# Half tiles of 128 rows and a lead of four groups in the routed stage of a graph and expert kernel

## The chip, the cores and the metric

The kernel runs on one core of one Trainium2 chip. The metric is the device time of one launch in microseconds, the median of a few runs; smaller is better. Beside the timed runs there is one profiled execution, with a trace of every instruction and transfer, from which all rows below come.

## The reference

```python
x = x + gnn(layernorm(x), edges, ...)      # two RGCN layers over 10000 nodes, 5000 edges, 512 wide
x = x + moe(layernorm(x), ...)             # on every one of the 10000 rows:
#   shared = gelu(t @ sw1.T + sb1) @ sw2 ...           2 shared experts, 64 wide each
#   top_v, top_i = top_k(softmax(t @ gate_w.T + gate_b), 2)       of 8 experts
#   routed = sum over the two picked experts of top_v * (gelu(t @ rw1[e].T + rb1[e]) @ rw2[e] + rb2[e])
```

The change lies wholly in the second line, the experts.

## The kernel before

The graph layers are not touched. Then comes the routed stage. The 10000 rows are handled twice: as 20 **groups** of 512 rows (128 partitions x QT = 4), in order of the nodes, and as **tiles** of 256 rows (FW), in order of the experts that they need.

A group q is loaded from x (`load_group`, SyncE's queue SP), z, the result of the graph layers, is added to it by an accumulating transfer (`add_z`, GpSimd), and it gets its statistics (`q_stats`, VectorE), its root (`group_rstd`, GpSimd), its normalisation (`q_norm`, ScalarE, L1336), its transposes (`q_transpose`, TensorE, L1593) and its router logits. VectorE finds the two experts of each row (`route_a`, `route_b`), which of six **kinds** (pairs of neighbouring experts, `KINDS`) the row belongs to (`sort_kinds`), and from counts made on TensorE its place (`positions`). Then `sort_rows` scatters the rows to `sorted_rows` in DRAM, one region a kind (L1119, four scatters a group).

A tile is 256 consecutive rows of one kind. `pick_tile(i)` (VectorE) chooses the kind of which most rows are ready and writes four integers to `pick_int`: the first row, the slot of the up weights in a chain of eight expert pairs (`CHAIN`), and two chunks of the down weights. There are always NF = 45 tiles, as many as the worst split over six kinds can need. `load_tile` reads them by a register (L846, L847). TensorE turns the tile (`turn_tile`, L1637, L1633), multiplies it by the picked up weights (`up_routed`), and by the shared ones (`up_shared`). ScalarE takes the gelu (L1372), VectorE multiplies it by the rows' shares (`weigh`, L2184), TensorE turns the result (`turn_hidden`, L1670), ScalarE and VectorE split it into a high and a low part (`routed_hi`; `routed_lo`, which writes grl, L2193), and TensorE multiplies it by the down weights (`down_first`, `down_routed`). `store_tile` scatters the rows to the output. All multiplications go through the helper at L1467, three for each product.

Slot i of the loop `for i in range(NF)` holds tile i and, on each engine in an order written out by hand, steps of a group some way ahead: even slots count, turn and normalise, odd ones route (`turned_in_slot`, `routed_in_slot`, `ranked_in_slot`). The first LEAD_GROUPS = 5 groups are done ahead of the loop. Four of them have the buffers stage0q to stage3q, the fifth has stage4q, which lies over the tile buffers xt2 and xt3; so `load_tile(2)` waits for the sort of group 4. Ahead of its first gelu ScalarE has `q_norm(5)`.

On TensorE the registers are loaded inside the slot, between the turn of the shares ("x") of the next tile and the last product of this one:

```python
                down_routed(i, 0, chunks)                 # waits for s_grl
                if exists(i + 1):
                    turn_tile(i + 1, "x")
                    chosen = picked(i + 1)                # three value_loads, L1737
                down_routed(i, 1, chunks)
```

The two calls are the two halves (128 rows each) of the tile; both use the same slot and chunks. `weigh` is called twice a slot, once for each chunk, on both halves at a time; VectorE loads its two chunks by registers too (L2258).

## Time and profile before

| | |
|---|---|
| runs, us | 1600.15, 1600.99, 1612.06; median 1600.99 |
| profiled execution, us | 1598.47, of which its span is 1596.7 |
| mean granted TensorE clock | 0.98 of full |
| busy, of the span | TensorE 93%, VectorE 58%, ScalarE 44%, GpSimd 41% |

The span runs from the first to the last instruction of the trace. "Idle before, releaser" in a row is the time for which an engine stood ahead of an instruction and what ended it; "issue" means that nothing the profile shows was waited for. PE is TensorE's matmuls, PEld its weight loads, PEldq and SPq the instructions in the queues of TensorE and SyncE. PEclk is the granted TensorE clock in tenths or shares of full speed, 2.4 GHz.

### The profile page before, as it was taken

The page shows a single profiled execution, that of the slowest core. Times are in us where ns is not written, and L with a number is a line of the kernel's source. Part 1 is how long each engine was busy: PE and PEld are TensorE (multiplying, and loading weights), DVE is VectorE, ACT ScalarE, POOL GpSimd, SP SyncE. Part 2 cuts the span into 40 slices and gives each one's busy share as a digit, 9 for nine tenths or more (in the row PEclk, how much of TensorE's full clock was granted, in tenths as well). Part 3 has the DMA queues.
Part 4 walks back from the last instruction along what each step waited for, and adds up shares of the span by engine and source line. Part 5 has one row for each costly group of instructions (what it writes and reads, how often), then busy time and mean ns, then how long its engine had stood idle before and what let it go on. Part 6 is the DMA issues. An engine that isn't in the chain of part 4 may idle for free. (4 is left out here: it accounts for less than half of the span.)

```text
span 1596.7 us, 27768 instructions
## 1 busy us (share of the span) xinstructions
PE 1491.6 (93%) x8680; PEld 1200.0 (75%) x8680; DVE 927.9 (58%) x2667; ACT 705.7 (44%) x1231; POOL 662.6 (41%) x989
## 2 busy tenths in 40 slices
PE   6999998989898999999999986599999999999997
PEld 4777666777786677777888864478888888888986
DVE  5555686867752333334766556566666767665453
ACT  3334334556652212122666535446565656453322
POOL 3762232457753000000467634546546464543222
PEclk9999999999999999999999998699999999999999
DMA  9999999597757999999667688879776776534220
GB/s 243 277 279 286 298 294 304 190 289 131 128 91 170 295 290 279 278 292 272 157 126 133 106 214 175 236 204 249 224 233 191 221 213 200 167 129 131 93 75 3
DMA packets 130212, 325.95 MB, mean 204 GB/s; under 512 B 17115, under 2 KB 17641, under 8 KB 129698
## 3 DMA queue, kind: packets, MB, share of 16 engines
q1 hardware_dynamic: 84626, 211.19, 44.8%
q0 software_dynamic: 45456, 113.12, 31.1%
q8 instruction: 70, 1.15, 0.3%
q14 instruction: 60, 0.49, 0.1%
HBM read 205.62 MB, written 121.74 MB: 205 GB/s over the span
## 5 line engine op out<-in xcount | busy, mean ns | idle before, releaser
L1207 ACT ACTIVATE th<-bank 128x512 fp32r<-128x512 f32 x158 | 94.2, 597 | 291.7 <-PE bank L1487 291.6
L1005 POOL DMA_INDIRECT gx<-y,dst_slot x42 | 46.2, 1101 | 266.1 <-ACT xn_e L1227 243.0
L1842 DVE SCALAR_TENSOR_TENSOR tl<-bank,th 128x512 fp32r<-128x512 f32 x79 | 54.4, 689 | 162.3 <-ACT th L1207 162.0
L1139 POOL DMA_INDIRECT out<-xt,out_row x90 | 93.2, 1035 | 128.4 <-DVE xt L2198 92.3
L1467 PE MATMUL bank<-root2h,th 128*128 128x512 f32 x316 | 133.1, 421 | 12.6 <-DVE tl L1842 7.8
L1467 PE MATMUL bank<-root1h,th 128*128 128x512 f32 x316 | 131.6, 416 | 7.9 <-DVE yout L1869 4.8
L1869 DVE TENSOR_TENSOR yout<-bank,bias_b 128x512 f32<-128x512 f32 x150 | 102.3, 682 | 45.4 <-DMA y<-yout 18.7
L1467 PE MATMUL bank<-root2l,th 128*128 128x512 f32 x316 | 126.0, 399 | 0.0
L1467 PE MATMUL bank<-root2h,tl 128*128 128x512 f32 x316 | 125.2, 396 | 0.0
L1467 PE MATMUL bank<-root1l,th 128*128 128x512 f32 x316 | 125.0, 396 | 0.0
L1467 PE MATMUL bank<-root1h,tl 128*128 128x512 f32 x316 | 124.1, 393 | 0.0
L1845 DVE TENSOR_TENSOR tl<-bank,th 128x512 fp32r<-128x512 f32 x79 | 54.3, 687 | 85.3 <-ACT th L1207 84.9
L1467 PE MATMUL bank<-w1qh,tth 128*128 x360 | 102.2, 284 | 1.6 <-issue 1.6
L1467 PE MATMUL bank<-w1ql,tth 128*128 x360 | 102.4, 284 | 0.0
L1467 PE MATMUL bank<-w1qh,ttl 128*128 x360 | 102.1, 284 | 0.0
L1500 PE MATMUL bank<-same,eh 128*128 128x256 f32 x336 | 84.9, 290 | 15.0 <-issue 8.8
L2184 DVE TENSOR_TENSOR gelr<-gelr,xt 128x256 f32<-128x256 f32 x90 | 34.4, 422 | 108.2 <-ACT gelr L1372 108.0
L1020 POOL DMA_INDIRECT z<-msg,scat_slot x42 | 71.3, 1697 | 61.2 <-issue 61.2
L1020 POOL DMA_INDIRECT y<-msg,scat_slot x42 | 72.1, 1716 | 52.3 <-issue 50.8
L1243 ACT ACTIVATE msg<-bank 128x512 f32<-128x512 f32 x84 | 49.2, 590 | 80.4 <-DMA z<-msg,scat_slot 36.5
L1501 PE MATMUL bank<-same,el 128*128 128x256 f32 x336 | 83.6, 286 | 0.0
L1500 PEld LDWEIGHTS bank<-same,eh 128*128 128x128 f32 x336 | 65.0, 194 | 23.1 <-issue 22.1
(355 smaller groups left out, 4378.8 us busy)
## 6 DMA issues: line engine op xcount, KB each, us to landing
basis_t<-in_gnn_basis SPq DMA_DIRECT2D x64, 896.0 KB
xt<-sorted_rows SPq DMA_DIRECT2D x45, 560.0 KB, 3.9
xin<-in_x SPq DMA_DIRECT2D x39, 512.0 KB, 8.8
xin<-y SPq DMA_DIRECT2D x39, 512.0 KB, 8.5
y<-yout SPq DMA_DIRECT2D x37, 512.0 KB, 9.2
z<-yout SPq DMA_DIRECT2D x34, 512.0 KB, 8.4
stage1q<-in_x SPq DMA_DIRECT2D x5, 1024.0 KB, 7.5
stage2q<-in_x SPq DMA_DIRECT2D x5, 1024.0 KB, 8.7
```

Of the source, the lines that this page charges most:

```text
L1005: pool.indirect_dma_start(out=gx[:, e % 6, :], out_offset=None, in_=x if pr.phase == SB else y1, in_offset=bass.IndirectOffsetOnAxis(ap=ds ...
L1020: pool.indirect_dma_start(out=y1 if pr.phase == SB else z, out_offset=bass.IndirectOffsetOnAxis(ap=scat_slot[:, t:t + 1], axis=0), in_=msg ...
L1139: pool.indirect_dma_start(out=out, in_=xt[i % 4][:, j, 0:H], in_offset=None, out_offset=bass.IndirectOffsetOnAxis(ap=out_row[:, i % 4, j:j ...
L1207: act.activation(th_a[:, s, :], tpb[s][:], f).then_inc(s_hi, 1)
L1243: act.activation(msg[:, e % 4, :], outb[(pr.T + j) % 2][:], ACT.Copy).then_inc(s_msg, 1)
L1467: ins = pe.matmul(out_ap, a(k), b(k), start=first, stop=last)
L1500: pe.matmul(o, eh[:, j, k * P:(k + 1) * P], m, start=j == 0, stop=False)
L1501: ins = pe.matmul(o, el[:, j, k * P:(k + 1) * P], m, start=False, stop=j == 1)
L1842: ins = dve.scalar_tensor_tensor(out=tl_a[:, s, :], in0=tpb[s][:], scalar=0.0, in1=th_a[:, s, :].bitcast(F32), op0=ALU.max, op1=ALU.subtract)
L1845: ins = dve.tensor_tensor(tl_a[:, s, :], tpb[s][:], th_a[:, s, :].bitcast(F32), ALU.subtract)
L1869: dve.tensor_tensor(target, out_bank(st)[:], bias_b[st.layer][:], ALU.add).then_inc(s_y, 1)
L2184: dve.tensor_tensor(part, part, share.to_broadcast([P, 2, 2, P // 2]), ALU.mult).then_inc(s_gs, 1)
```

## The change

Each tile is now two **halves** of 128 rows, each picked, loaded, and multiplied by weights of its own. A kind's region is padded by 128 rows and not 256, and there are 42 tiles. So there are two picks a tile (`pick_half`), two transfers of 128 rows, six register loads on TensorE (slot and two chunks for each half), four on VectorE and two on SyncE; `down_routed` and `up_routed` take each half's own. `weigh` runs four times, on a half and a chunk. The matmuls of a tile are the same in number and size.

The lead is four groups. stage4q goes, and with it the special waits. x of group 4 is loaded behind the load of tile 0 on SP, and its z is added by GpSimd behind the sort of group 2. All distances between a slot and the group that is worked on in it shrink by one group. On VectorE `positions(0)` now comes ahead of the statistics of group 3, and `group_of_pick` lets tile 0 depend on groups 0 and 1.

The core of the diff (the remaining parts set constants, tables and semaphore counts for halves, and move the same steps on further engines):

```diff
@@ -107,11 +107,11 @@
...
     HEAD = 3 * P
-    KIND = FW + N
+    KIND = P + N
     XROWS = HEAD + NKIND * KIND
-    NF = (N + NKIND * (FW - 1)) // FW
+    NF = ((N + NKIND * (P - 1)) // P + 1) // 2
     FAR = 1.0e6
-    LEAD_GROUPS = 5
+    LEAD_GROUPS = 4
@@ -284,9 +287,7 @@
...
         xt3, x5 = place("xt3", [P, 2, XW], at=x4)
-        stage4q, x6 = place("stage4q", [P, QT, XW], at=x3)
-        assert x6 == x5
-        stage = (stage1q, stage2q, stage0q, stage3q, stage4q)
+        stage = (stage1q, stage2q, stage0q, stage3q)
         xt = (xt0, xt1, xt2, xt3)
@@ -561,16 +562,11 @@
...
-            return stage[q if q < LEAD_GROUPS else (q - 1) % 4]
+            return stage[q % 4]
...
-            if q == LEAD_GROUPS - 1:
-                eng.wait_ge(s_tp, 2 * (NT + ET))
-            elif LEAD_GROUPS <= q < LEAD_GROUPS + 4:
-                eng.wait_ge(s_sorted[q - LEAD_GROUPS], 16 * QT)
-            else:
-                wait(eng, s_sorted[q % 4], 16 * QT * (q // 4))
+            wait(eng, s_sorted[q % 4], 16 * QT * (q // 4))
@@ -582,7 +578,7 @@
...
-            return min(NQ - 1, (i + 5) // 2)
+            return min(NQ - 1, (i + 3) // 2)
@@ -595,23 +591,23 @@
         def turned_in_slot(i):
-            return group_at(i, 10)
+            return group_at(i, 8)
         def routed_in_slot(i):
-            return group_at(i, 9)
+            return group_at(i, 7)
         def ranked_in_slot(i):
-            q = (i + 8) // 2
+            q = (i + 6) // 2
             return q if i % 2 == 0 and q < NQ else None
...
                 return [t for t in (i + 3, i + 4) if t < NF]
-            return [i + 4] if i > 2 * NQ - 10 and i + 4 < NF else []
+            return [i + 4] if i > 2 * NQ - 8 and i + 4 < NF else []
         def logit_bank(q):
-            return bank[1] if q in (1, 3) else bank[7]
+            return bank[1] if q in (0, 2) else bank[7]
@@ -843,9 +838,9 @@
...
                     sp.wait_ge(s_ost[i % 4], 32 * (i // 4))
-                r = sp.value_load(pick_int[0:1, i, 0:1], min_val=0, max_val=XROWS - FW)
-                sp.dma_start(xt[i % 4][:], sorted_rows[bass.ds(r, FW), :].rearrange("(p j) w -> p j w", j=2))\
-                    .then_inc(s_xt[i % 4], 16)
+                for j in range(2):
+                    r = sp.value_load(pick_int[0:1, 2 * i + j, 0:1], min_val=0, max_val=XROWS - P)
+                    sp.dma_start(xt[i % 4][:, j, :], sorted_rows[bass.ds(r, P), :]).then_inc(s_xt[i % 4], 16)
@@ -856,20 +851,18 @@
...
                     load_group(3)
+            sp.wait_ge(s_pads, 16 * NKIND)
+            load_tile(0)
             load_group(4)
             load_group(5)
-            sp.wait_ge(s_pads, 16 * 2 * NKIND)
-            load_tile(0)
+            load_tile(1)
             load_group(6)
-            load_tile(1)
-            load_group(7)
-            sp.wait_ge(s_sorted[0], 16 * QT * 2)
             load_tile(2)
...
                     load_tile(i + 3)
-                if group_at(i, 15) is not None and group_at(i, 15) > 7:
-                    load_group(group_at(i, 15))
+                if group_at(i, 13) is not None and group_at(i, 13) > 6:
+                    load_group(group_at(i, 13))
             for i in range(4):
@@ -1122,10 +1115,10 @@
...
                 pool.wait_ge(s_pick, i + 1)
-                pool.wait_ge(s_xt[i % 4], 16 * (i // 4 + 1))
-                pool.tensor_tensor(hidden_part[:], pick[:, i, 4:5], pick[:, i, 0:1], ALU.subtract).then_inc(s_rows, 1)
+                pool.wait_ge(s_xt[i % 4], 32 * (i // 4 + 1))
+                pool.tensor_tensor(hidden_part[:], pick[:, 2 * i:2 * i + 2, 4], pick[:, 2 * i:2 * i + 2, 0], ALU.subtract).then_inc(s_rows, 1)
                 pool.wait_ge(s_rows, 4 * i + 1)
-                pool.tensor_scalar(far_row[:], row_index[:], hidden_part[:, 0:1], FAR, ALU.is_lt,
+                pool.tensor_scalar(far_row[:], hidden_part[:], row_index[:, 0:1], FAR, ALU.is_gt,
                                    ALU.mult).then_inc(s_rows, 1)
@@ -1149,35 +1142,32 @@
...
                 add_z(q)
-            for q in range(4):
-                if q == 3:
-                    add_z(4)
+            for q in range(3):
                 group_rstd(q)
...
             sort_rows(1)
+            group_rstd(3)
+            group_extras(3)
             sort_rows(2)
+            add_z(4)
+            group_rstd(4)
             add_z(5)
-            group_rstd(4)
-            group_extras(4)
-            sort_rows(3)
-            group_rstd(5)
-            add_z(6)
             rows_of_tile(0)
...
                 if q is not None:
-                    if q > 4:
+                    if q > 3:
                         group_extras(q)
                     sort_rows(q)
-                if group_at(i, 14) is not None and group_at(i, 14) > 6:
-                    add_z(group_at(i, 14))
+                if group_at(i, 12) is not None and group_at(i, 12) > 5:
+                    add_z(group_at(i, 12))
                 if i:
...
                     rows_of_tile(i + 1)
-                if group_at(i, 11) is not None and group_at(i, 11) > 5:
-                    group_rstd(group_at(i, 11))
+                if group_at(i, 9) is not None and group_at(i, 9) > 4:
+                    group_rstd(group_at(i, 9))
                 if 0 < i <= len(LATE2_PAIRS) + 1:
@@ -1403,32 +1393,26 @@
...
                 q_full(1, k)
+            q_exp(0)
+            q_logits(1)
             q_norm(2, range(2))
-            q_exp(0)
+            q_exp(1)
             q_norm(2, range(2, QT))
-            q_logits(1)
             for k in range(KC):
                 q_full(2, k)
-            q_exp(1)
             q_logits(2)
-            q_norm(3, range(2))
-            q_exp(2)
-            q_norm(3, range(2, QT))
-            for k in range(KC):
-                q_full(3, k)
-            q_logits(3)
             for n in range(FC + E_SPLITS, SPLITS):
                 expert_hi(n)
-            q_exp(3)
-            q_norm(4)
+            q_exp(2)
+            q_norm(3)
             for part in ("a", "b"):
...
             for k in range(KC):
-                q_full(4, k)
-            q_logits(4)
-            q_exp(4)
-            q_norm(5)
+                q_full(3, k)
+            q_logits(3)
+            q_exp(3)
+            q_norm(4)
             for i in range(NF):
@@ -1665,8 +1649,7 @@
...
                 for c, j in itertools.product(range(2), range(2)):
-                    if j == 0:
-                        pe.wait_ge(s_gs, 2 * i + c + 1)
+                    pe.wait_ge(s_gs, 4 * i + 2 * c + j + 1)
                     ins = pe.transpose(b[:, c * FW + j * P:c * FW + (j + 1) * P], gelr[:, j, c * P:(c + 1) * P], ident[:])
@@ -1708,40 +1691,41 @@
...
             logits(0)
-            for q in (1, 2):
-                q_transpose(q, 0)
-                q_transpose(q, 1)
-                logits_by_token(q - 1)
-                if q > 1:
-                    count_ranks(q - 2)
-                q_transpose(q, 2)
-                q_transpose(q, 3)
-                logits(q)
+            q_transpose(1, 0)
+            q_transpose(1, 1)
+            logits_by_token(0)
+            q_transpose(1, 2)
+            q_transpose(1, 3)
+            logits(1)
+            logits_by_token(1)
+            count_ranks(0)
+            q_transpose(2, 0)
+            q_transpose(2, 1)
+            count_ranks(1)
+            q_transpose(2, 2)
+            q_transpose(2, 3)
+            logits(2)
             logits_by_token(2)
-            count_ranks(1)
             count_ranks(2)
+            for part in ("a", "b", "x"):
+                turn_tile(0, part)
             turn_group(3)
...
             logits_by_token(3)
-            count_ranks(3)
-            for part in ("a", "b", "x"):
-                turn_tile(0, part)
-            turn_group(4)
-            logits(4)
-            logits_by_token(4)
             pe.wait_ge(s_ewl, FC + 1 + len(CHAIN))
...
                 tops = (len(CHAIN) - 2, FC - 1, FC - 1)
-                return [pe.value_load(pick_int[0:1, i, c:c + 1], min_val=int(c > 1), max_val=tops[c - 1]) for c in (1, 2, 3)]
+                return [[pe.value_load(pick_int[0:1, 2 * i + j, c:c + 1], min_val=int(c > 1), max_val=tops[c - 1])
+                         for c in (1, 2, 3)] for j in range(2)]
...
                 q_turn, q_route, q_rank = turned_in_slot(i), routed_in_slot(i), ranked_in_slot(i)
-                slot, chunks = chosen[0], chosen[1:]
+                chunks = [row[1:] for row in chosen]
                 for j in range(2):
-                    ins = up_routed(i, j, slot)
+                    ins = up_routed(i, j, chosen[j][0])
                 ins.then_inc(s_upr, 1)
@@ -2166,9 +2148,16 @@
...
                                               op0=ALU.is_equal, op1=ALU.mult))
-                link(dve.tensor_reduce(pick[:, i, :], pick_all[:], AX_X, ALU.add))
-                dve.tensor_copy(pick_int[0:1, i, :], pick[0:1, i, 0:4])
+                dve.tensor_reduce(pick[:, n, :], pick_all[:], AX_X, ALU.add)
                 link(dve.tensor_tensor(last, last, pick_all[:, 5, :], ALU.add))
+
+            def pick_tile(i):
+
+                q = group_of_pick(i)
+                dve.wait_ge(s_qpos, q + 1)
+                for j in range(2):
+                    pick_half(2 * i + j, q)
+                link(dve.tensor_copy(pick_int[0:1, 2 * i:2 * i + 2, :], pick[0:1, 2 * i:2 * i + 2, 0:4]))
                 dve.sem_inc(s_pick, 1)
@@ -2177,11 +2166,11 @@
...
-            def weigh(i, c, chunk):
+            def weigh(i, c, j, chunk):
                 dve.wait_ge(s_ger, i + 1)
-                part = gelr[:, :, c * P:(c + 1) * P].rearrange("p j (e f) -> p j e f", e=2)
-                share = xt[i % 4][:, :, bass.ds(2 * chunk + (WHOLE - 2), 2)].rearrange("p j (e a) -> p j e a", a=1)
-                dve.tensor_tensor(part, part, share.to_broadcast([P, 2, 2, P // 2]), ALU.mult).then_inc(s_gs, 1)
+                part = gelr[:, j:j + 1, c * P:(c + 1) * P].rearrange("p j (e f) -> p (j e) f", e=2)
+                share = xt[i % 4][:, j:j + 1, bass.ds(2 * chunk + (WHOLE - 2), 2)].rearrange("p j (e a) -> p (j e) a", a=1)
+                dve.tensor_tensor(part, part, share.to_broadcast([P, 2, P // 2]), ALU.mult).then_inc(s_gs, 1)
@@ -2218,51 +2207,45 @@
...
                     q_stats(1, range(QT))
-            dve.wait_ge(s_tp, 2 * (NT + ET))
-            row_columns(stage4q).then_inc(s_qs, 1)
             q_stats(2, range(QT))
             route_a(0)
-            q_stats(3, range(QT))
             route_b(0)
...
             sort_kinds(1)
+            positions(1)
+            pick_tile(0)
+            q_stats(3, range(QT))
             route_a(2)
-            positions(1)
+            for n in range(FC + E_SPLITS, SPLITS):
+                expert_lo(n)
             route_b(2)
...
             positions(2)
-            pick_tile(0)
-            q_stats(4, range(QT))
-            route_a(3)
-            for n in range(FC + E_SPLITS, SPLITS):
-                expert_lo(n)
-            route_b(3)
-            sort_kinds(3)
-            positions(3)
             pick_tile(1)
...
                 f_lo(0, part)
-            q_stats(5, range(QT))
-            route_a(4)
-            route_b(4)
-            sort_kinds(4)
+            q_stats(4, range(QT))
+            route_a(3)
+            route_b(3)
+            sort_kinds(3)
             for i in range(NF):
-                q_route, q_rank, q_first, q_more = routed_in_slot(i), ranked_in_slot(i), group_at(i, 12), group_at(i, 11)
+                q_route, q_rank, q_first, q_more = routed_in_slot(i), ranked_in_slot(i), group_at(i, 10), group_at(i, 9)
                 if i:
...
                         f_out(i - 1, j)
-                chunks = [dve.value_load(pick_int[0:1, i, c:c + 1], min_val=1, max_val=FC - 1) for c in (2, 3)]
-                for c in range(2):
-                    weigh(i, c, chunks[c])
+                chunks = [[dve.value_load(pick_int[0:1, 2 * i + j, c:c + 1], min_val=1, max_val=FC - 1) for c in (2, 3)]
+                          for j in range(2)]
+                for c, j in itertools.product(range(2), range(2)):
+                    weigh(i, c, j, chunks[j][c])
                 if q_rank is not None:
...
                 routed_lo(i)
-                if q_more is not None and q_more > 5:
+                if q_more is not None and q_more > 4:
                     q_stats(q_more, range(2, QT))
```

## Rows read from the trace of the kernel before

**Rows 1.** The page, busy time of each engine: us, share of the span, instructions.
```profile
PE 1491.6 (93%) x8680; PEld 1200.0 (75%) x8680; DVE 927.9 (58%) x2667; ACT 705.7 (44%) x1231; POOL 662.6 (41%) x989
```

**Rows 2.** The gelu by its line, four stretches: count, ns min/median/max, first to last start.
```profile
L1372 ACT ACTIVATE gelr<-bank x4: 597/597/599, 1034.9 to 1078.2; 128x512 f32<-128x512 f32 x4
L1372 ACT ACTIVATE gelr<-bank x3: 597/597/597, 1104.3 to 1130.6; 128x512 f32<-128x512 f32 x3
L1372 ACT ACTIVATE gelr<-bank x19: 597/597/599, 1144.5 to 1377.2; 128x512 f32<-128x512 f32 x19
L1372 ACT ACTIVATE gelr<-bank x13: 598/598/600, 1448.8 to 1579.7; 128x512 f32<-128x512 f32 x13
```

**Rows 3.** Stretches: us, busy PE, PEld, DVE, ACT, POOL (x), PEclk, DMA share, GB/s.
```profile
505.00:509.00 4.00, 3.59 (x9) 2.89 (x10) 0.91 (x2) 0.00 (x0) 0.00 (x0) 0.57 1.06 267
923.00:927.00 4.00, 4.00 (x19) 3.31 (x18) 0.00 (x0) 0.60 (x1) 2.25 (x2) 1.00 0.17 13
1010.00:1020.00 10.00, 0.67 (x10) 0.59 (x11) 6.33 (x33) 2.93 (x4) 6.64 (x12) 0.50 0.96 207
1054.00:1059.00 5.00, 5.00 (x21) 4.10 (x20) 3.29 (x21) 1.09 (x2) 3.73 (x11) 0.66 0.43 121
1423.00:1500.00 77.00, 77.00 (x515) 68.85 (x514) 43.14 (x133) 25.50 (x52) 24.00 (x46) 1.00 0.35 119
```

**Rows 4.** The chain that ended last, ahead of slot 0: start, us, what.
```profile
993.12 1.13 POOL sorted_rows L1119
...
1007.98 5.35 DMA sorted_rows<-stage0q,pos
...
1015.84 3.82 DMA xt<-sorted_rows
```

**Rows 5.** Timeline, 1022 to 1032 us: start, us, engine, line, operation.
```profile
1022.94 2.46 DVE L2078 BATCH_NORM_STATS2 qbn<-stage1q 128x6 f32<-128x512 f32 x4
...
1027.63 0.24 POOL L1088 TENSOR_SCALAR qnmr<-qnmr 128x4 f32<-128x4 f32 x1
...
1030.43 2.21 ACT L1336 ACTIVATE stage1q<-stage1q,qnmr,qrstd 128x512 f32<-128x512 f32 x3
```

**Rows 6.** Transfers, 930 to 1100 us: count, KB each, median us to landing.
```profile
stage1q<-in_x SPq DMA_DIRECT2D x3, 1024.0 KB, 7.5
...
stage1q<-z POOLq DMA_DIRECT2D x2, 1024.0 KB, 8.8
stage2q<-z POOLq DMA_DIRECT2D x2, 1024.0 KB, 13.5
...
stage4q<-in_x SPq DMA_DIRECT2D x1, 1024.0 KB, 14.9
```

**Rows 7.** Timeline of TensorE, three idles and what ended them.
```profile
503.25 0.95 PE L1487 MATMUL bank<-ident,xin 128*128 128x128 f32 x7 [2.26 <-DMA xin<-y]
...
922.40 0.49 PE L1467 MATMUL bank<-wrh,th_b 128*128 x1 [2.21 <-ACT msg L1243]
...
1053.39 0.87 PE L1637 MATMUL bank<-ident,xt 128*128 128x128 f32 x6 [2.36 <-DMA xt<-sorted_rows]
```

**Rows 8.** TensorE's queue, 1441 to 1446 us, by lines: ns min/median/max, first to last start.
```profile
L1737 PEldq TENSOR_LOAD <-pick_int x3: 296/298/466, 1442.0 to 1443.4; - x3
L1737 PEldq FUSED_REGOPS  x3: 146/151/151, 1442.5 to 1443.8; - x3
L1467 PEldq FUSED_REGOPS  x6: 46/46/51, 1441.3 to 1445.4; - x6
```

**Rows 9.** Timeline of TensorE's weight loads behind two sets of register loads.
```profile
1112.94 0.19 PEld L1467 LDWEIGHTS bank<-w2h,grh 128*128 128x128 f32 x1 [1.09 <-issue]
...
1444.05 0.19 PEld L1467 LDWEIGHTS bank<-w2h,grh 128*128 128x128 f32 x1 [0.20 <-issue]
```

**Rows 10.** Timeline of VectorE in the same two plain slots.
```profile
1440.61 0.69 DVE L2193 TENSOR_TENSOR grl<-bank,grh 128x512 fp32r<-128x512 f32 x1
...
1449.60 0.76 DVE L2184 TENSOR_TENSOR gelr<-gelr,xt 128x256 f32<-128x256 f32 x2 [3.11 <-ACT gelr L1372]
```

More of the change, by code:

```diff
@@ L176, in gnn_moe_kernel @@
         e_scan = sb("e_scan", [ER, EC])
+        e_f_at = top[0]
         e_f = sb("e_f", [ER, 4, EC])
@@ L824, in _ @@
             for k in range(NKIND):
-                for j in range(2):
-                    first = HEAD + k * KIND + j * P
-                    sp.dma_start(sorted_rows[first:first + P, :], zeros[:]).then_inc(s_pads, 16)
+                first = HEAD + k * KIND
+                sp.dma_start(sorted_rows[first:first + P, :], zeros[:]).then_inc(s_pads, 16)
             walk(sp, SC, step)
@@ L1452, in _ @@
                     q_exp(q_route)
-                q = group_at(i, 11)
-                if q is not None and q > 5:
+                q = group_at(i, 9)
+                if q is not None and q > 4:
                     q_norm(q)
@@ L1764, in _ @@
                     q_transpose(q_turn, 3)
-                down_routed(i, 0, chunks)
+                down_routed(i, 0, chunks[0])
                 if exists(i + 1):
@@ L1768, in _ @@
                     chosen = picked(i + 1)
-                down_routed(i, 1, chunks)
+                down_routed(i, 1, chunks[1])
         @block.vector
@@ L2155, in positions, with pick_half @@
                     link(dve.tensor_tensor(posf[:, 0:n], posf[:, 0:n], again_row[:], ALU.add))
-                dve.tensor_scalar(pos[:, q % 4, 0:n], posf[:, 0:n], float(FW), None, ALU.add).then_inc(s_qpos, 1)
-            def pick_tile(i):
-                q = group_of_pick(i)
-                dve.wait_ge(s_qpos, q + 1)
+                dve.tensor_scalar(pos[:, q % 4, 0:n], posf[:, 0:n], float(P), None, ALU.add).then_inc(s_qpos, 1)
+            def pick_half(n, q):
                 limit, far, last = lim[:, q % 2, 0, :], lim[:, q % 2, 1, :], kinds[:, 4, :]
@@ L2273, in _ @@
                     pick_tile(t)
-                if q_first is not None and q_first > 5:
+                if q_first is not None and q_first > 4:
                     q_stats(q_first, range(2))
```

20 lines of the change are left out of this document (11 added, 9 removed).

## The prediction

> **What bounds the kernel now.** I read the page first, then stretches by stage, then single tiles. The page has TensorE busy for 93% of the span [rows 1]. The change touches only the last stage, the 45 routed tiles with the token groups woven in. So the questions are what one tile costs there, and what leaves the array idle.
>
> The gelu of a tile marks its slot. In the last slots, which carry no group work, 12 periods lie between 1448.8 and 1579.7 [rows 2]: 10.91 us a tile. Where groups are woven in, 18 periods lie between 1144.5 and 1377.2 [rows 2]: 12.93 us, or 25.86 a pair. One group costs 25.86 - 21.82 = 4.04 us. TensorE is busy for 77.00 of 77.00 us there [rows 3]: this stage is its own, and whatever leaves its array idle is paid in full.
>
> Ahead of slot 0 it is different. From 1010 to 1020 the array works 0.67 us of 10, and the granted clock is 0.50 [rows 3]: a chain of transfers and small VectorE, GpSimd and ScalarE work.
>
> **The change, part by part.**
>
> *Three tiles less.* NF goes from (10000 + 6 x 255) // 256 = 45 to ((10000 + 6 x 127) // 128 + 1) // 2 = 42. The slots that go are plain: 3 x 10.91 = 32.7 us less.
>
> *One group more in the loop.* The lead is four groups, not five, so 16 are woven in, not 15: 4.0 us more.
>
> *The lead-in.* Tile 0 needs two groups sorted, not three. VectorE comes to the positions of group 0 some 4 us earlier, since the statistics of group 3 (2.5 us, like those of rows 5) and the columns of stage4q no longer stand ahead of them. So the first sort, now at 993.12 [rows 4], starts near 989. Its 12 scatters issue 1.35 us apart ((1007.98 - 993.12) / 11), and the last lands 5.35 us after its start [rows 4]: the eighth lands at 989 + 7 x 1.35 + 5.35 = 1003.8. From landing to the issue of tile 0 SyncE took 2.5 us (1013.33 to 1015.84 [rows 4]); so tile 0 goes out near 1006, 10 us earlier. Slot 0 does not gain these 10 us, because ScalarE has the normalisation of the next group ahead of the first gelu, and that group, number 4, is late next. Its x is now queued on SP behind tile 0, at 1007. Such loads take 7.5 us to land, in a crowd 14.9; z, which GpSimd adds behind it, 8.8 to 13.5 [rows 6]. Then stand in a row VectorE's statistics and GpSimd's root (1022.94 to 1027.87, 4.9 us), and from the start of four normalisations to the gelu 1034.9 - 1030.43 = 4.5 us [rows 2, 5]. So the first gelu comes between 1007 + 7.5 + 8.8 + 9.4 = 1032.7 and 1007 + 14.9 + 13.5 + 9.4 = 1044.8. Now it is at 1034.9 [rows 2]. I take 1035, nearer the low end, as fewer transfers stand beside it: no shift, ends -2 and +10. Queued behind the waiting statistics on VectorE are the routing of group 3 and the weighting of tile 0; the picks of tiles 0 to 2 are done ahead.
>
> What does go is a wait just behind. Tile 2 waits for the sort of group 4, since its buffer lies in stage4q; TensorE stood 2.36 us for it [rows 7], and the clock of the next 5 us was 0.66 [rows 3]. The gelus of tiles 0 to 3 lie 43.3 us apart in three slots, where 3 x 12.93 = 38.8 would do [rows 2]. Without stage4q I take 4 of these 4.5 us off. Lead-in together: -4 us, ends -6 and +8.
>
> *Six register loads for three.* This is the large term. `picked(i + 1)` (L1737) stands between the turn of the shares and `down_routed(i, 1)`. It loads three registers a tile; with a slot and two chunks for each half it loads six. Each is a TENSOR_LOAD of 0.298 us, a FUSED_REGOPS of 0.151 and a short SEQ_ASSERT in TensorE's own queue, 0.65 us from one to the next (1442.5 to 1443.8 over two) [rows 8]. The queue begins them at 1442.0, just after VectorE's grl (1440.61 + 0.69 [rows 10]), for which `down_routed(i, 0)` waits; it cannot begin sooner. The last ends at 1444.0, and the next weights go in at 1444.05, after 0.20 us of "issue" [rows 8, 9]. So the first three use up all the cover there is, and three more are bare: 3 x 0.64 = 1.9 us. Besides, `down_routed(i, 1)` now addresses other chunks than `down_routed(i, 0)` and can't reuse their address work: one FUSED_REGOPS of 0.046 us [rows 8] and the operation behind it, with gaps some 0.2 us, bare; the rest of the new address work lies under running matmuls. Sum 2.1 us, 41 times: 86 us. (The loads for tile 0 lie under the wait for group 4.) Low end 1.8 us (74), if the array lags a little more; high end 2.4 (98), since some sets take longer: one left 1.09 us idle and not 0.20 [rows 9].
>
> The Trainium skill ("TensorE: Matmul & The Clock Gate", Part 1, "Architectural detail") gives TensorE's queue a depth of 64. By that it could hold some 32 pairs of weights and matmul, more than these loads need, and their price would be nothing. The 0.20 us of [rows 9] speaks against it here: the queue stops for a semaphore before it is full.
>
> *What is given back.* In every second slot TensorE waits a little for the normalised rows and for a gelu behind its table load. Around the set that left 0.89 us more idle, the gelus 1104.3 to 1130.6 span 26.3 us to the pair, 0.45 over 25.86 [rows 2, 9]: the other 0.45 was absorbed. 16 x 0.45 = 7 us less, ends 0 and -10.
>
> *Four smaller multiplications for two* (L2184). Two take 0.76 us in a row [rows 10], 0.38 each for 256 columns. With 128 I take 0.23: 0.9, so 0.15 us more, on the path only in the nine plain slots: 1 us. VectorE's own loads, four for two, are at 0.65 each 1.3 us more, ahead of this multiplication; it idles 3.11 us there [rows 10]. In even slots the picks, four halves for two tiles, add 2.5 us of small operations. 3.8 us then stand against 3.11 and the 2.1 by which each slot grows: it fits, narrowly. The two transfers of 280 KB for one of 560 have 3.82 us to landing [rows 4], several slots ahead of need.
>
> *The clock.* The array now idles for 2 us in each slot. After an idle of 2.26 us and one of 2.36 us [rows 7] the granted clock of the next stretch was 0.57 and 0.66; after one of 2.21 us it stayed 1.00 [rows 3, 7]. The lower level is 1.2 GHz; the stretch of 5 us at 0.66 lacks 0.34 x 5 = 1.7 us, about what one fall costs. My idles are a little shorter and each lies between matmuls, so I take a third of 41: 13 falls of 1.6 us, 20 us. Ends 0 and 40.
>
> **Sum.** -32.7 + 4.0 - 4 + 86 - 7 + 1 + 20 = +67 us. The profiled execution took 1598.47 us, all but 1.8 of it its span. That gives 1665.8. The median of the runs, 1600.99, stands 2.5 us above that execution, so a median could be 1668; I say 1667.
>
> **Rivals.**
>
> *The clock holds.* The same without the 20 us: 1647. For it: the idle of 2.21 us. Against it: the other two of rows 7. 0.25.
>
> *The loads are hidden.* Faster. If the queue could begin the six loads 4 us ahead of the array and not 2, neither they nor the clock would cost anything: 1598.5 - 32.7 + 4.0 - 4 + 1 = 1567. It decides at 0.77 us bare a tile (31.7 us over 41); below that the change wins. Against it are the 0.20 and 1.09 us of "issue" [rows 9]: a longer set was bare at once. 0.07. The queue depth that the Trainium skill states in "TensorE: Matmul & The Clock Gate", Part 1, would allow this case.
>
> *VectorE becomes the bound of the even slots.* Picks and loads outrun the room by about 1 us in each of 16 pairs: 1683. For it: 3.8 us added against 3.11 idle. Against it: TensorE's slots grow by 2.1. 0.07.
>
> *The change doesn't do what it says.* The trip count is fixed in the program; excluded.
>
> **How the numbers follow.** My forecast, the clock falling some of the time, holds 0.58 and reaches by its terms from 1650 to 1692; clock holding 0.25; hidden 0.07; VectorE 0.07; some cover I don't see leaves about 0.8 us bare, 0.03. The range 1634 to 1692 takes in the first, the second and most of the fourth. Faster by over 1% (about what a measurement of this kernel can tell from no change) 0.07, within 1% 0.03, slower 0.90.
>
> **What would show it.** Of the changed kernel: 42 gelus, the plain ones 13.0 us apart or more, not 10.9; six TENSOR_LOADs a tile in TensorE's queue, and behind them an idle of 2 us named "issue"; a pair with a group at 29.6 us or more; stretches of the last stage with PEclk under 1, or not; the first gelu near 1035 and no wait for tile 2. I am wrong if the plain period is near 11, which would mean that the loads moved under matmuls; the lead-in is wrong if the first gelu is under 1030 or over 1042.

## The result, and the profile after

| | before | after |
|---|---|---|
| median, us | 1602.9 (4 runs beside it) | 1656.95 (4 runs, 1655.4 to 1659.6) |
| profiled execution, us | 1598.47 | 1657.01 |
| its span | 1596.7 | 1655.3 |

The ratio after to before is 1.033, with a 95% interval of 1.028 to 1.037. The change makes the kernel 54 us slower.

Busy time of each engine on the page of after, which answers to [rows 1], and two groups of its fifth part (busy us, mean ns of one, then the idle of the engine just before):

```profile
PE 1483.0 (90%) x8464; PEld 1191.9 (72%) x8464; DVE 961.9 (58%) x2954; ACT 703.2 (42%) x1212; POOL 649.7 (39%) x971
...
L1451 PE MATMUL bank<-w2h,grh 128*128 x168 | 75.8, 451 | 76.5 <-issue 76.5
...
L2173 DVE TENSOR_TENSOR gelr<-gelr,xt 128x128 f32<-128x128 f32 x168 | 37.9, 286 | 128.5 <-ACT gelr L1362 101.0
```

TensorE does less work than before and takes longer for it. A single group of matmuls, the first of each down product, has 76.5 us of idle before it, all of it "issue": nothing that the profile shows as a producer was late.

The gelu by its line (count, ns, first to last start), three stretches of after; these answer to [rows 2]:

```profile
L1362 ACT ACTIVATE gelr<-bank x3: 597/598/598, 1024.0 to 1056.4; 128x512 f32<-128x512 f32 x3
...
L1362 ACT ACTIVATE gelr<-bank x19: 597/598/599, 1149.5 to 1425.7; 128x512 f32<-128x512 f32 x19
...
L1362 ACT ACTIVATE gelr<-bank x9: 598/600/600, 1533.8 to 1638.7; 128x512 f32<-128x512 f32 x9
```

With groups woven in, 18 periods take 276.2 us: 30.69 us a pair, where before had 25.86. The last eight take 104.9 us: 13.1 each, where before had 10.91; the first of them carries a fall of the clock (14.5 us), the other seven are 12.8 to 13.0. The first gelu comes at 1024.0, 10.9 us earlier than before.

TensorE's queue in the last slot of after that routes a group (L1720 are the register loads; this answers to [rows 8]), then the timeline of its weight loads and of its matmuls behind them ([rows 9]):

```profile
L1720 PEldq TENSOR_LOAD <-pick_int x6: 296/300/302, 1509.6 to 1512.9; - x6
L1720 PEldq FUSED_REGOPS  x6: 146/146/151, 1510.0 to 1513.2; - x6
```
```profile
1513.60 0.19 PEld L1451 LDWEIGHTS bank<-w2h,grh 128*128 128x128 f32 x1 [1.86 <-issue]
```
```profile
1513.60 0.49 PE L1451 MATMUL bank<-w2h,grh 128*128 x1 [1.63 <-issue]
```

Six loads, five steps of 0.65 us (1509.6 to 1512.9), the last done at about 1513.4; the array has nothing from 1511.97 to 1513.60. In the slots behind it, from 1556 on, which have no group work, the same idle is 1.70 to 1.88 us.

In the slots with a group every second idle is longer. Four of them on the timeline of TensorE, then stretches of after (us, busy PE, PEld, DVE, ACT, POOL (x), PEclk, DMA share, GB/s; they answer to [rows 3]):

```profile
1035.89 0.49 PE L1451 MATMUL bank<-w2h,grh 128*128 x1 [2.02 <-issue]
...
1051.58 0.49 PE L1451 MATMUL bank<-w2h,grh 128*128 x1 [1.65 <-issue]
...
1067.13 0.49 PE L1451 MATMUL bank<-w2h,grh 128*128 x1 [2.41 <-issue]
...
1098.10 0.49 PE L1451 MATMUL bank<-w2h,grh 128*128 x1 [2.25 <-issue]
```
```profile
1098.00:1102.00 4.00, 3.90 (x14) 3.40 (x15) 3.16 (x5) 0.00 (x0) 3.39 (x7) 0.57 1.07 175
...
1509.00:1514.00 5.00, 3.37 (x17) 2.55 (x16) 2.67 (x16) 2.31 (x5) 0.00 (x0) 1.00 0.43 116
...
1149.00:1426.00 277.00, 244.03 (x1635) 209.28 (x1635) 180.77 (x765) 137.39 (x236) 124.17 (x225) 0.96 0.62 177
```

Behind the idle of 2.25 us the granted clock fell to its lower level, 1.2 GHz, for 3.4 us (0.57 over the 4 us of the row); behind 1.63 us it stayed 1.00. There are 16 such falls between the first gelu and the last. From 1030 to 1192 there are eleven idles of this kind: of the six of 2.02 to 2.41 us five were followed by a fall, of the five of 1.50 to 1.66 us none. Over the whole loop, 15 of the 17 idles of 2.0 us and more were followed by one, and of the 22 between 1.3 and 1.9 us one was, that of 1.84 us at 1541.96.

What one fall costs can be read off the same trace. Of two long slots one behind the other, the first has a fall (at 1160.0) and the second has none, though an idle of 2.16 us stood in it (ScalarE's timeline, where each gelu marks a slot):

```profile
1149.49 0.60 ACT L1362 ACTIVATE gelr<-bank 128x512 f32<-128x512 f32 x1 [0.24 <-PE bank L1640]
1166.34 0.60 ACT L1362 ACTIVATE gelr<-bank 128x512 f32<-128x512 f32 x1 [8.05 <-PE bank L1640]
...
1180.54 0.60 ACT L1362 ACTIVATE gelr<-bank 128x512 f32<-128x512 f32 x1 [0.33 <-PE bank L1640]
1195.86 0.60 ACT L1362 ACTIVATE gelr<-bank 128x512 f32<-128x512 f32 x1 [6.53 <-PE bank L1640]
```

They take 16.85 and 15.32 us. Of the 13 long slots from tile 6 to tile 30, the 11 with a fall have a mean of 16.8 us, the two without one 15.3; so a fall costs 1.5 us.

### The profile page after: what moved, and what is told of

The parts are those of the page before. It is cut to its first block and busy times, and to the rows that moved or that the text cites. A ratio compares the mean times of both kernels' runs of the same rounds, so it can differ in the third digit from the quotient of the medians.

```text
span 1655.3 us, 28927 instructions
## 1 busy us (share of the span) xinstructions
PE 1483.0 (90%) x8464; PEld 1191.9 (72%) x8464; DVE 961.9 (58%) x2954; ACT 703.2 (42%) x1212; POOL 649.7 (39%) x971
## 5 line engine op out<-in xcount | busy, mean ns | idle before, releaser
L1451 PE MATMUL bank<-w2h,grh 128*128 x168 | 75.8, 451 | 76.5 <-issue 76.5
L1132 POOL DMA_INDIRECT out<-xt,out_row x84 | 86.5, 1030 | 117.1 <-DVE xt L2187 95.4
L2173 DVE TENSOR_TENSOR gelr<-gelr,xt 128x128 f32<-128x128 f32 x168 | 37.9, 286 | 128.5 <-ACT gelr L1362 101.0
L1362 ACT ACTIVATE gelr<-bank 128x512 f32<-128x512 f32 x42 | 25.1, 598 | 192.5 <-PE bank L1640 192.3
L1451 PE MATMUL bank<-w1ql,tth 128*128 x336 | 99.6, 296 | 0.0
L1451 PEld LDWEIGHTS bank<-w2h,grh 128*128 128x128 f32 x168 | 33.5, 200 | 91.2 <-issue 86.0
L1484 PE MATMUL bank<-same,eh 128*128 128x256 f32 x336 | 85.1, 290 | 13.9 <-DVE el L1888 7.7
## 6 DMA issues: line engine op xcount, KB each, us to landing
stage1q<-in_x SPq DMA_DIRECT2D x5, 1024.0 KB, 6.8
stage2q<-in_x SPq DMA_DIRECT2D x5, 1024.0 KB, 9.5
```

The lines of the kernel that those rows point to most:

```text
L1132: pool.indirect_dma_start(out=out, in_=xt[i % 4][:, j, 0:H], in_offset=None, out_offset=bass.IndirectOffsetOnAxis(ap=out_row[:, i % 4, j:j ...
L1451: ins = pe.matmul(out_ap, a(k), b(k), start=first, stop=last)
L1484: pe.matmul(o, eh[:, j, k * P:(k + 1) * P], m, start=j == 0, stop=False)
L2173: dve.tensor_tensor(part, part, share.to_broadcast([P, 2, P // 2]), ALU.mult).then_inc(s_gs, 1)
```

## The experiments

All times are medians. Ratios are to runs of the kernel before on the same chip (their median is 1597 to 1599 us, for after 1602.9 us). "Loop" is from the first gelu to the last in the profiled execution.

| kernel | TensorE / VectorE loads a tile | us | ratio, 95% | first gelu | loop |
|---|---|---|---|---|---|
| before | 3 / 2 | 1598 | 1 | 1034.9 | 544.8 |
| after | 6 / 4 | 1656.95 | 1.033 (1.028-1.037) | 1024.0 | 614.6 |
| e1_split | 3+3 / 4 | 1630.0 | 1.021 (1.017-1.025) | 1025.6 | 588.1 |
| e2_three_loads | 3 / 4 | 1584.2 | 0.991 (0.988-0.995) | 1027.4 | 542.2 |
| e3_before_six | 6 / 2, 45 tiles | 1699.6 | 1.063 (1.059-1.068) | 1034.6 | 649.8 |
| e4_fill | 6 / 4, array kept busy | 1644.0 | 1.029 (1.026-1.033) | 1027.5 | 598.1 |
| e5_three_two | 3 / 2 | 1561.6 | 0.978 (0.973-0.982) | 1029.2 | 515.0 |
| e6_spread_both | 3+1+1+1 / 1+1+1+1 | 1576.8 | 0.986 (0.981-0.990) | 1025.1 | 532.8 |
| e7_before_42 | 3 / 2, 42 tiles | 1562.5 | 0.977 (0.973-0.982) | 1029.1 | 513.4 |
| e9_quiet | 3 / 4, small group transfers | 1566.8 | 0.981 (0.978-0.984) | 1027.1 | 520.8 |
| e10_lead | as e6, group 4 earlier | 1587.6 | 0.994 (0.991-0.997) | 1037.0 | 540.2 |
| e11_spread_pe | 3+1+1+1 / 4 | 1585.8 | 0.994 (0.991-0.996) | 1021.8 | 542.3 |
| e12_two_dve | 6 / 2 | 1652.7 | 1.035 (1.031-1.040) | 1025.2 | 610.9 |

The kernel e8_group_first has a single run, 1658.1 us, and is used for its trace alone.

### Are the loads the cost?

**Three loads less in after (e2), three more in before (e3).**

```diff
-return [[pe.value_load(... 2 * i + j, c ...) for c in (1, 2, 3)] for j in range(2)]
+row = [pe.value_load(... 2 * i, c ...) for c in (1, 2, 3)]
+return [row, row]
```
```diff
-return [pe.value_load(pick_int[0:1, i, c:c + 1] ...) for c in (1, 2, 3)]
+rows = [[pe.value_load(pick_int[0:1, i, c:c + 1] ...) for c in (1, 2, 3)] for j in range(2)]
+return rows[0]
```

> The kernel after, with TensorE loading only the three registers of half 0 and using them for half 1 too (half 1's products then use half 0's experts, so that the output is not the reference's); every other instruction, the four weighings and VectorE's four loads among them, is kept. Theory: the three loads less are 1.9 us a tile and nearly all of them lay bare: 1657 - 42 x 1.9 - 22 for the clock falls = about 1555, plain tiles 10.9 to 11.1 us apart. Rival (weighings and VectorE's loads carry a part): plain tiles stay over 11.5 and the time over 1590.

> The kernel before, with three register loads more for each tile on TensorE, whose values nobody uses; nothing else changed. Theory: 44 x 2.0 us = 88 us more, and some clock falls, 0 to 30 us: 1691 to 1720, plain tiles 12.9 us apart. Rival (the loads by themselves are covered, and it is the halves that cost): 1603 to 1615.

e3 gave +101 us for 44 sets, 2.3 us each, nothing else touched: within the range and near what its theory says. This includes 15 falls of the clock. In its profile the plain tiles without a fall stand 12.7 to 12.9 us apart. e2 took some 67 us off after (0.042 x 1598) and is faster than before. (e2 leaves out more than the loads: both halves then have one address, so the new address work of the second half goes too. e3 adds loads alone, and its plain tiles, 12.8 us at the mean against 12.9 in after, leave about 0.1 us a tile for that work.) Its plain tiles are 10.9 to 11.0 us apart, as expected, but the total is 29 us above the 1555 that I had given. The gelus by stretches say where:

```profile
L1362 ACT ACTIVATE gelr<-bank x19: 597/598/600, 1140.8 to 1392.8; 128x512 f32<-128x512 f32 x19
...
L1362 ACT ACTIVATE gelr<-bank x9: 598/598/600, 1481.6 to 1569.6; 128x512 f32<-128x512 f32 x9
```

The pairs with a group take 28.0 us, not 25.9: single slots alternate 12.1 and 15.8, where before has 12.0 and 13.9. In one of the long slots, VectorE's queue (L2241, its register loads), VectorE's timeline, and the stretch:

```profile
L2241 DVEq TENSOR_LOAD <-pick_int x4: 521/1174/1668, 1178.6 to 1183.0; - x4
```
```profile
1184.56 0.70 DVE L2174 TENSOR_TENSOR gelr<-gelr,xt 128x128 f32<-128x128 f32 x3 [3.44 <-issue]
```
```profile
1178.50:1184.50 6.00, 4.87 (x39) 3.69 (x38) 2.59 (x4) 2.18 (x4) 4.50 (x8) 1.00 0.99 169
```

The gelu was done at 1181.4; the first weighing starts at 1184.56, behind 3.44 us of "issue". VectorE's four loads took from 1178.6 to 1184.4. A second bound had lain behind the first: from 1060 to 1420 TensorE waited 13 times for a weighing, 17.6 us in all.

### VectorE's loads

**Two of VectorE's four loads left out (e5 from e2, e12 from after).** Both weigh half 1 with half 0's registers; the four weighings stay.

```diff
-chunks = [[dve.value_load(... 2 * i + j, c ...) for c in (2, 3)] for j in range(2)]
+row = [dve.value_load(... 2 * i, c ...) for c in (2, 3)]
+chunks = [row, row]
```

> As e2_three_loads, and VectorE too loads only half 0's two registers and uses them for half 1's two weighings (output not the reference's, as there); the four weighings are kept. In e2 the gelus of the slots that load a group stayed 1.9 us too far apart (15.8 us where the kernel before has 13.9), and VectorE's four loads there took 5.8 us with 3.4 us of issue ahead of the first weighing. Theory (VectorE's register loads are the second cost, in the slots with a group): e2's 1584 - 17 x 1.9 = 1552, between 1543 and 1562, the long slots back near 13.9. Rival (it is the four weighings or GpSimd's work on them): 1580 or more.

> The kernel after with one thing less: VectorE loads only half 0's two registers and weighs half 1 with them too (output not the reference's); TensorE's six loads and the four weighings stay. In e2 against e5 these two loads were worth 23 us once TensorE had three loads. Theory (beside six loads on TensorE they lie in the shadow: in after the last of the four ended 0.17 us ahead of the first weighing): 1650 to 1660, as after. Rival (the two costs add up, each in its own slots): about 1630.

The gelus of e5, the stretch with groups and the last nine:

```profile
L1362 ACT ACTIVATE gelr<-bank x19: 597/597/599, 1136.3 to 1370.1; 128x512 f32<-128x512 f32 x19
...
L1362 ACT ACTIVATE gelr<-bank x9: 598/598/600, 1456.8 to 1544.2; 128x512 f32<-128x512 f32 x9
```

Pairs are 26.0 us and plain tiles 10.9: VectorE's two extra loads cost 22 us of time (0.991 to 0.978) and 27 us of loop once TensorE has three. Beside TensorE's six they cost nothing (1.035 against 1.033, intervals overlapping). They lie in the shadow, as e12's theory said; adding the two up would have been wrong. In after the last of the four ends close to the first weighing (by line L2240, then the timeline of VectorE):

```profile
L2240 DVEq TENSOR_LOAD <-pick_int x4: 429/714/1601, 1162.9 to 1166.9; - x4
L2240 DVEq FUSED_REGOPS  x4: 183/186/190, 1164.6 to 1167.4; - x4
L2240 DVEq SEQ_ASSERT  x4: 23/23/23, 1164.8 to 1167.6; - x4
```
```profile
1167.79 0.90 DVE L2173 TENSOR_TENSOR gelr<-gelr,xt 128x128 f32<-128x128 f32 x4 [4.12 <-ACT gelr L1362]
```

The profile puts the idle of 4.12 us down to the gelu, which had ended at 1166.94; the last load ended at 1167.62.

e5's loop also clears the other suspects. It has the four weighings, the picks by halves and one group more, and takes 515.0 us; that of e7, the kernel before cut to 42 tiles, takes 513.4. e7 has the wait for tile 2 (its first two slots are 4.6 us longer than e5's) and one group less (4.0 us), so all that is left for weighings and picks is some 2 us.

**What makes a load slow (e9).** In e2's trace I set each of VectorE's 156 loads from 1060 us on beside the share of the DMA engines that was busy while it ran: with a share under 0.2 there are 59, mean 0.31 us, the longest 0.52; with 0.8 and more there are 85, mean 0.76, the longest 1.67.

```diff
+n, h = (1, 64) if 7 <= q < NQ - 1 else (tiles_of(q), H)
...
-sp.dma_start(stage_of(q)[:, 0:tiles_of(q), 0:H], q_rows(x, q)) ...
+sp.dma_start(stage_of(q)[:, 0:n, 0:h], q_rows(x, q)[:, 0:n, 0:h]) ...
```

The addition of z is cut in the same way.

> As e2_three_loads, with VectorE's four loads kept, but from group 7 to the last but one only 64 columns of one tile of x and z are brought in, not four whole tiles (output not the reference's); instructions, waits and order are the same. In e2's trace a register load of VectorE took 0.30 us while the DMA engines were quiet and up to 1.7 us in the slots in which a group arrives. Theory (the transfers slow the loads): VectorE's loads fall to 0.3 to 0.5 us there, their 1.9 us in 17 slots go, 1584 - 27 = about 1557, as in e5 with two loads only. Rival (VectorE's own work, or GpSimd's stores in front, slow them): they stay over 1 us and the time 1575 to 1585.

VectorE's loads, first those of e2 and then those of e9, in the stretch with groups:

```profile
L2241 DVEq TENSOR_LOAD <-pick_int x66: 296/304/1668, 1139.8 to 1364.8; - x66
```
```profile
L2243 DVEq TENSOR_LOAD <-pick_int x72: 296/300/581, 1145.1 to 1368.7; - x72
```

The longest fell from 1.67 to 0.58 us, the long slots from 15.8 to 13.8 us, the time to 1566.8, about 10 us over the theory's 1557. The instructions are the same; only bytes are gone. So the transfers slow the loads. e9's time is 5 us over e5's, and its first plain tiles stood at 12.4 to 12.8 us; why is open.

### Can the loads be covered?

**Half 1's three loads elsewhere (e1), then one by one (e6, e11).**

Of e1, where `picked(i, j)` loads the three of one half:

```diff
     ins = up_routed(i, j, chosen[j][0])
 ins.then_inc(s_upr, 1)
+if exists(i + 1):
+    second = picked(i + 1, 1)
...
 turn_tile(i + 1, "x")
-chosen = picked(i + 1)
+chosen = [picked(i + 1, 0), second]
```

Of e6 and e11:

```diff
 ins.then_inc(s_upr, 1)
+second = [picked_one(i + 1, 1, 1)]
...
 up_shared(i)
+second.append(picked_one(i + 1, 1, 2))
 turn_hidden(i)
...
+second.append(picked_one(i + 1, 1, 3))
 down_routed(i, 0, chunks[0])
```

In e6 VectorE's four loads for tile i + 1 also stand singly: ahead of `f_lo(i + 1, "a")`, between it and `"b"`, behind `route_a`, and behind the picks.

> The kernel after, with TensorE's six register loads in two places: the three of the next tile's half 0 where they were (behind the turn of x), the three of its half 1 behind the up projection of the chosen experts, where the engine's queue is about 2 us ahead of its array. Theory (the time went into register loads that lie bare, and into the clock falls behind them): both threes are covered by work already in the queue, plain tiles come 10.9 to 11.3 us apart instead of 12.9, the pairs with a group about 25 to 27, hardly a clock fall is left; 1657 - 42 x 1.8 - 22 = about 1559, between 1545 and 1580. Rival (it is the four weighings, or VectorE's four loads): nothing of that moves, over 1640. Rival (a load costs its time wherever it stands): about 1657 too, the idle only moves behind the up projection.

> The kernel after with the same loads, nothing left out: TensorE's three of the next half 0 stay behind the turn of x; those of half 1 stand one by one behind the up projection of the chosen experts, behind the shared one, and ahead of the down product of half 0; VectorE's four for the next tile stand one by one behind the routed remainder of this tile and later, instead of in front of the weighings. Theory (a load costs only what lies beyond the work already in the queue; in e1 three together fell into the same us as VectorE's four, and both took up to 1.8 us each): single loads are covered in most places; between 1560 and 1605. Rival (the queue doesn't get ahead again between the places, or a load of 1.5 us is bare anywhere): 1625 or more, no better than e1.

> e6_spread_both with VectorE's four loads back in front of the weighings; TensorE's spread as in e6. It divides e6's gain. Theory (two engines, each with its own bare loads, the second seen only when the first is gone): TensorE's part alone gives 1577 + 17 x 1.9 = 1609 (1600 to 1618). Rival (VectorE's place doesn't matter once TensorE's loads are single): 1577 to 1585.

e1 fits none of its three cases: 1630. Plain tiles improved to 11.5 us, short of 11.3. The pairs stayed at 30.6 (12.2 and 18.4), and 13 falls of the clock are in the loop, one in nearly every long slot. One long slot of e1: TensorE's three moved loads, VectorE's four, what the weight loads then waited for, and the stretch.

```profile
L1720 PEldq TENSOR_LOAD <-pick_int x3: 1139/1497/1577, 1102.2 to 1106.0; - x3
```
```profile
L2242 DVEq TENSOR_LOAD <-pick_int x4: 850/1152/1491, 1101.8 to 1106.4; - x4
```
```profile
1107.53 0.19 PEld L1587 LDWEIGHTS bank<-tfull,gwp 128*32 128x32 f32 x8 [3.75 <-issue]
```
```profile
1102.00:1107.00 5.00, 1.99 (x17) 1.78 (x15) 2.27 (x4) 0.60 (x1) 4.08 (x8) 1.00 1.06 181
```

The two sets ran in the same 5 us, under a DMA share of 1.06, and a load took 1.1 to 1.6 us, not 0.30. My expectation priced a moved load by the row of a quiet place. Whether the other engine's loads add to the slowness is open: they overlap transfers in every case here.

The gelus of e6, the stretch with groups and the last nine:

```profile
L1362 ACT ACTIVATE gelr<-bank x19: 597/597/599, 1139.1 to 1379.9; 128x512 f32<-128x512 f32 x19
...
L1362 ACT ACTIVATE gelr<-bank x9: 598/600/600, 1469.6 to 1557.8; 128x512 f32<-128x512 f32 x9
```

e6 is in the range of its theory: 1576.8 us, pairs of 26.8, plain tiles of 10.9 to 11.0 at the end. It leaves nothing out, and beats before by 1.4% (0.981 to 0.990) and after by some 75 us (0.047 x 1598). e11, with TensorE's loads spread alone, has 1585.8, below the 1600 to 1618 of its theory and next to the 1577 to 1585 of its rival: VectorE's place is worth 12 us (0.994 to 0.986), not 32. In e11 TensorE still waits for weighings, but from 1060 to 1420 for 8.3 us in all, where e2 has 17.6.

### The clock

**Work in the idle (e4).**

```diff
 rows[j].append(pe.value_load(...))
+if i and (j, c) != (1, 3):
+    pe.matmul(downb[1][:, 0:P], ident[:], zeros[:, 0:P], start=False, stop=False)
```

> The kernel after, with a matmul of zeros (128 columns, added into the bank that waits for half 1's down product) behind each of the first five loads of a tile. The loads are as they were, only the array isn't idle all through them. Theory (idle of 2.1 us and more lowers the granted clock, some 17 times, 1.5 us each): the falls go, the distance of plain tiles stays 12.9, the pairs with a group come 29.6 apart instead of 30.7: 1657 - 25 = 1632. Rival (the falls come from something else): 17 falls stay and 1657, or a little more for the added work.

Stretch with groups of e4, beside the one of after above (PEclk 0.96):

```profile
1150.00:1420.00 270.00, 260.45 (x1824) 224.31 (x1823) 181.47 (x768) 138.81 (x238) 123.97 (x225) 1.00 0.63 182
```

No fall is left from the first gelu to the last, and plain tiles stay at 12.9 to 13.1. So idle arrays brought the falls, and the loads cost what they cost without them. The pairs go from 30.69 to 29.82, and the profiled loop is 16.5 us shorter. The total is 12 us over the theory's 1632: by ratios e4 is only 6 us under after (1.033 and 1.029, intervals overlapping).

The 16.5 us understate the falls, because the added matmuls cost something too: e4's long slots take 15.4 us and its plain ones 13.0, where those of after without a fall take 15.3 and 12.9. By the slots of after, 16 falls of 1.5 us are 24 us. Of the 99.6 us by which the loop of after exceeds that of e5, the clock is therefore 16 to 24 us by the traces, which the medians are too coarse to confirm, and the loads themselves are the other 76 to 83. The lower figure agrees with the 76.5 us of "issue" ahead of the down products on the page.

### Tiles and lead-in

**42 tiles in the kernel before (e7).** `NF` as in after; the last rows are not computed.

> The kernel before, cut after 42 of its 45 tiles (the rows of the last three aren't computed, so the output isn't the reference's). It prices the three tiles by themselves: 3 x 10.91 = 32.7 us less by the prediction's first term, 1600 - 33 = 1567 (1563 to 1571). Rival (the last tiles also hide the stores, which then lie bare): 1572 to 1580.

36 us less (0.977, interval 29 to 44), with a plain distance of 10.9 in its trace: the 32.7 stand within the uncertainty. The profiled loops differ by 31.4.

**Group 4 first on SyncE (e8), and on GpSimd too (e10).** e8 swaps `load_tile(0)` and `load_group(4)`; e10 does this to e6 and also puts `add_z(4)` ahead of `sort_rows(2)`.

> The kernel after with x of group 4 loaded ahead of tile 0, not behind it. In its profile x(4) was asked for at 996.3 us, 1.5 us behind the first half of tile 0, and the stats of group 4 waited for z added to it. Theory (that transfer gates the first gelu): the first gelu 1.5 us earlier against the sort of group 0, the rest as in after. Rival (the table and the turn of tile 0 gate it): first gelu unchanged against that sort.

> e6_spread_both and an earlier group 4: on SP its x ahead of tile 0, on GpSimd z added to it ahead of the scatter of group 2, not behind. In e8 x(4) asked for 7 us earlier left the first gelu at 42.9 us behind the first sort, as in after (42.6). Theory (z(4) gates the first gelu, and GpSimd's queue sets when it is asked for): z(4) about 5 us earlier, the first gelu 3 to 5 us earlier, tile 1's pick hardly later: e6's 1577 - 4 = 1573. Rival (the later scatter of group 2 holds back tiles 1 and 2): the gain is given back by slot 3, 1577.

VectorE's timeline and a part of the chain of after:

```profile
1014.77 2.47 DVE L2062 BATCH_NORM_STATS2 qbn<-stage1q 128x6 f32<-128x512 f32 x4 [11.12 <-DMA stage1q<-z]
```
```profile
1002.16 0.96 POOL sorted_rows L1112
1003.12 11.63 DMA stage1q<-z
1014.77 0.04 DVE qbn L2062
```

z(4) gates the first gelu in after, as predicted, and in e8 as well: with x(4) asked for at 989.28 us its z still goes out behind the scatters of group 2, at 1004.08, and the first gelu comes 42.9 us behind the first sort, as in after (42.6). That is the rival's number in e8's text, but for another reason, which e10's text then named. e10 did send z(4) ahead of those scatters, and lost: tile 0 now took 7.3 us to land beside it, where such tiles took 3.2 at the median in after, and TensorE waited 11.5 us for it (chain and timeline of e10).

```profile
1009.38 7.30 DMA xt<-sorted_rows
1016.68 0.04 issue
1016.73 0.47 PE bank L1621
```

The first gelu came 46.8 us behind the first sort (990.2 to 1037.0), and the time is 11 us over e6's. Neither of my two outcomes. z(4) did go out earlier, 14.5 us behind the first sort and not 22.6 as in e6. But the second half of tile 0 was asked for 19.2 us behind that sort (1009.38), in e6 14.5, and then landed in 7.3 us, in e6 in 4.4. So tile 0 had become the gate. Both lags fit transfers that share the DMA engines; this was argued and not tested.

## Why the prediction came out right

It said slower, 1667 us, 1634 to 1692; measured 1657. Term by term:

- **Three tiles, -32.7:** right (e7: -36 with 29 to 44 by its time, -31.4 by its loop).
- **One group more in the loop, +4.0, and weighings, +1:** not separated. Both fit e5's loop, which beside e7's leaves some 2 us for weighings and picks.
- **Lead-in, -4:** mis-sized, in the one part that was put at nothing. The first gelu came at 1024.0, 10.9 us earlier, under the 1030 that the text named as its failure. The step that failed is "tile 0 goes out near 1006", and with it the x of group 4 "at 1007": they went out at 994.8 and 996.3. The first sort started at 981.4, not 989, the eight scatters landed sooner, and x(4) landed in 5.7 us. Over all profiles the first sort starts at 990.5 on average in the three kernels with the old lead and at 983.5 in the ten with the new one (e10, where group 4 goes first, left out), and the first gelu at 1032.9 and 1025.8; so about 7 us belong to the change and the other 4 us of this execution to the part ahead of it, which the change doesn't touch. The wait for tile 2, the -4 proper, is gone as forecast: the first four pairs of slots of before are 6.1 us longer than four pairs of 25.86, those of after 2.7 us longer than four of 30.69.
- **TensorE's loads, +86, of which 7 absorbed:** right in mechanism and size: 2.0 us a tile where the slot is plain (12.9 against 10.9), predicted 2.1, and 76 to 83 us over the loop, predicted 79. "A third load uses up the cover, three more are bare" is what e3 and e2 show.
- **VectorE's loads, hidden:** right for after by its total (e12), wrong in its price. I took 0.65 us a load from the quiet rows; in the slots where a group arrives the four took 4.3 to 5.6 us in after and up to 6.1 in e2. They were covered only because TensorE was late for its own reasons. The rival "VectorE becomes the bound" was thus true of the kernel one fix later.
- **Clock, +20 by 13 falls of 1.6 us:** 16 falls of 1.5 us, 24 us, of which e4 took back 16.5. The price of a fall was right and the count a little low; that about one idle in three would bring a fall was a guess, which came near.
- **Hidden loads, the rival at 0.07:** false in after, but e6 shows its core: with singles spread out, most of the cost of the loads goes (e6's loop is 82 us shorter than that of after, and 18 us longer than that of e5 with half the loads). The Trainium skill ("TensorE: Matmul & The Clock Gate", Part 1, "Architectural detail") gives the queue a depth of 64; in after the queue was about 2.4 us ahead of the array where the loads began (1509.6 against 1511.97), and nothing here shows that more of it could be used.

Loads and clock together were predicted at 86 - 7 + 20 = 99 us, and the loops of after and e5 differ by 99.6. The rest of the loop was predicted at -32.7 + 4 - 4 + 1 = -31.7, and the loops of e5 and before differ by -29.8. So in the profiled executions (58.6 us between the spans, +67 predicted) the error is nearly the lead-in alone: the first gelu came 10.9 us earlier than forecast. Some 4 of these are chance, a part of the kernel ahead of the change that ran faster in this execution. It is luck, too, that the smaller errors of the other terms offset each other.

## What to carry to other kernels

A register load is work of the queue that issues an engine's instructions: price it by the work already queued ahead of it, not by its own length, and spread loads singly over places where the queue is ahead. Price it in the neighbourhood where it will stand, since beside heavy transfers single ones took over five times as long (1.67 us against 0.30). When a cost is removed, look in the trace for the engine that arrived just in time before; here it took 27 us of loop back at once.

## What the runs showed of the hardware

- A register load from on-chip memory took 0.30 us, 0.64 us to the next with its register operations; the Trainium skill ("DMA: Bandwidth & Descriptors", "Latency and other measured facts") states a floor of some 600 ns for a tensor load. The instruction itself is below that here, 0.30 us; only the step with its register operations, 0.64 us, comes near it. Under a DMA share of about 1 a single one took up to 1.7 us, and with the transfers cut down (e9) at most 0.58 in the same stretch on VectorE.
- In after, idles of 2.0 us and more inside a busy stage were followed by 3.4 us at 1.2 GHz in 15 of 17 cases, those of 1.3 to 1.9 us in one of 22. The length alone doesn't decide: in before, the clock stayed at 1.00 behind 2.21 us, and in e2 it fell behind one of 1.7 us and stayed behind others of 1.6. A fall made a slot 1.5 us longer (16.8 against 15.3). Matmuls of zeros in the idle kept the clock at 1.00 (e4).
